# Expert tiles spread over the scan units: nine per chunk of eight, in a loop written out

## What is computed

```python
# branch 1: tokens sorted by nearest of 8 means, then a selective scan (d = 256 channels, 16 states)
dA = exp(d_t[..., None] * A)
h  = dA * h + (d_t * u_t)[..., None] * b_t[:, None, :]     # one step per token, state (256, 16)
y  = einsum('bdn,bn->bd', h, c_t)                          # then + D * u, and tokens put back in place
# branch 2: 8 experts, each token goes to 2 of them
logits = xt @ w_gate; top_logits, sel = top_k(logits, 2); probs = softmax(top_logits)
h = silu(xt @ w1[e]) * (xt @ w3[e]);  y = h @ w2[e];  out += probs * y
```

## Time and profile before

| | |
|---|---|
| median of 3 runs | 818.53 us (818.16 to 818.74) |
| profiled execution | 817.38 us |
| its span, first to last instruction | 815.3 us |
| busy over the span | PE 663.9 us (81%), DVE 682.9 (84%), POOL 597.3 (73%), ACT 431.0 (53%) |
| mean granted clock of TensorE | 0.913 of full speed |
| DMA | 118.63 MB, mean 146 GB/s |

### The profile page before, as it was taken

One profiled execution on the slowest core, in us unless ns is written; L12 is line 12 of the kernel. 1 busy time (PEld: TensorE's weight loads), 2 busy tenths in 40 slices (PEclk: granted clock), 3 DMA queues, 4 the chain that ended last, 5 costly groups with the idle time before them and its releaser, 6 DMA issues. The chain is left out here.

```text
span 815.3 us, 15751 instructions
## 1 busy us (share of the span) xinstructions
PE 663.9 (81%) x4538; PEld 422.7 (52%) x4539; DVE 682.9 (84%) x882; ACT 431.0 (53%) x926; POOL 597.3 (73%) x372
## 2 busy tenths in 40 slices
PE   3734889788998798989998898999889798989870
PEld 2523745245655465556655565565556555655550
DVE  5769777579999999999999999999999999997110
ACT  1324656465655556656655575566557554653320
POOL 3728800038788898988989898888989898889532
PEclk9866955599999989999999998999999998999995
DMA  7972659979944754674575466547645654662322
GB/s 228 371 259 91 180 206 297 321 221 241 210 102 103 144 118 87 146 150 94 115 163 111 89 149 138 105 90 164 139 90 125 134 127 90 142 142 35 49 27 26
DMA packets 76845, 118.63 MB, mean 146 GB/s; under 512 B 22456, under 2 KB 56848, under 8 KB 74512
## 3 DMA queue, kind: packets, MB, share of 16 engines
q1 hardware_dynamic: 54656, 90.95, 41.2%
q0 software_dynamic: 19824, 27.16, 19.4%
q10 hardware_dynamic: 2336, 0.15, 0.2%
HBM read 82.87 MB, written 35.27 MB: 145 GB/s over the span
## 5 line engine op out<-in xcount | busy, mean ns | idle before, releaser
L534 POOL TENSOR_TENSOR ring<-ring,bc 128x1024 f32<-128x1024 f32 (+2 forms) x128 | 308.0, 2424 | 38.9 <-DVE state L1047 38.0
L1044 DVE TENSOR_TENSOR_SCAN ring<-ring,state,pb 128x512 f32<-128x512 f32 x256 | 313.8, 1267 | 4.6
L654 ACT ACTIVATE ring<-late,aneg 128x512 f32<-128x512 f32 x256 | 164.2, 721 | 12.0 <-DMA late<-dd_d 9.1
L1035 DVE TENSOR_TENSOR pb<-fb,bc 128x1024 f32<-128x1024 f32 x128 | 157.3, 1229 | 3.0
L1284 PE MATMUL py<-w2x,pool 128*128 x568 | 141.6, 395 | 0.5 <-ACT pool L726 0.3
L1267 PE MATMUL fa<-w,pool 128*128 x284 | 137.7, 608 | 3.9 <-issue 2.8
L506 POOL DMA_INDIRECT out_dram<-pool,meta x71 | 112.9, 1590 | 29.8 <-issue 15.7
L1267 PE MATMUL fb<-w,pool 128*128 x284 | 134.3, 596 | 0.0
L486 POOL DMA_INDIRECT pool<-xn_d,meta x71 | 71.3, 1004 | 81.3 <-DVE ids L1001 33.5
L1284 PEld LDWEIGHTS py<-w2x,pool 128*128 128x128 f32 x568 | 107.7, 200 | 13.6 <-issue 1.0
L1267 PEld LDWEIGHTS fb<-w,pool 128*128 128x128 f32 x284 | 54.5, 192 | 68.9 <-issue 68.9
(11 more groups left out here) (213 smaller groups left out, 752.8 us busy)
## 6 DMA issues: line engine op xcount, KB each, us to landing
late<-dd_d SPq DMA_DIRECT2D x256, 128.0 KB
bc<-bc_d SPq DMA_DIRECT2D x72, 256.0 KB
w<-in_L_ffn_w_dram SPq DMA_DIRECT2D x16, 512.0 KB, 8.6
ring<-in_L_attn_x_dram SPq DMA_DIRECT2D x8, 512.0 KB, 4.3
out_dram<-ring SPq DMA_DIRECT2D x8, 512.0 KB, 7.7
xn_d<-w2x SPq DMA_DIRECT2D x8, 512.0 KB, 8.6
dd_d<-pool SPq DMA_DIRECT2D x8, 512.0 KB
dd_d<-ring SPq DMA_DIRECT2D x8, 512.0 KB, 5.1
```

What stands on the lines that cost most here:

```text
L534: ins = po.tensor_tensor(r, r, c_rows, ALU.mult)
L654: ins = ac.activation(ring[:, g % RING, n, :], dd[:, g % 2, 0, :], ACT.Exp, scale=aneg[:, NH * g + n:NH * g + n + 1])
L1035: ve.tensor_tensor(pb[:, :].rearrange("p (n c) -> p n c", n=2), pd[:, :].rearrange("p (o c) -> p o c", o=1).to_broadcast([P, 2, CH]), b_ro ...
L1044: ve.tensor_tensor_scan(r, r, pb[:, CH * m:CH * m + CH], state[:, NH * g + n:NH * g + n + 1], ALU.mult, ALU.add).then_inc(S["scan_done"], 1)
```

## The change

It takes the tiles into the units. Chunk 0 has tiles 0 to 7: unit 0 goes first and alone, units 1 to 7 have one tile each and unit 7 a second one in its middle, between its two halves on DVE. Each later chunk has nine tiles: one per unit and a second one in unit 3. So tile 70 belongs to unit 63 and none is left behind. Gathers run six tiles ahead instead of four (`XR`), `ye` has three buffers instead of two (`YE`), `ya` has two and replaces the copy into `yb`. The table's entries are loaded nine at a time. POOL adds two tiles in unit 5 of a chunk (`DOUBLE`), with the second gather and add between the halves of its multiplication. Half of the last unit's multiplication goes to DVE. Chunk 7's scan adds are issued together behind the last tile's. All loops of the stage are written out, with constants as semaphore targets. The first unit's exponentials wait for DVE's preparation to end and for their own load only; those of units 1 and 2 wait for the stores of the last factors, whose buffers they overwrite.

```diff
-SCAN_STEPS = (3, 3, 7, 7)
-REST_SCAN_STEPS = (1, 2, 3, 4)
-REST = range(SPI * NCH + 1, FT)
+UNITS = NCH * G
+SCAN_UNITS = {3: (0, 1), 7: (2, 3)}
+DOUBLE = 5
+XR, XT, YE = 6, 4, 3
+BLOCK = G + 1
...
+        def first_tile(u):
+            c, g = u // G, u % G
+            return u - 1 if c == 0 else BLOCK * c - 1 + g + (g >= G // 2)
+        def middle_tile(u):
+            c, g = u // G, u % G
+            if c == 0:
+                return u if g == G - 1 else None
+            return BLOCK * c + G // 2 - 1 if g == G // 2 - 1 else None
+        def experts_by(u):
+            c, g = u // G, u % G
+            return max(0, u - 1) if c == 0 else BLOCK * c - 1 + g + (g >= DOUBLE)
...
 POOL
+            for u in range(UNITS):
+                c, g = u // G, u % G
+                here = range(experts_by(u - 1) if u else 0, experts_by(u))
+                if len(here) and here[0] + XR < FT:
+                    gather(here[0] + XR)
+                scans = SCAN_UNITS.get(g, ()) if c else ()
+                split = 1 if scans else NH // 2
+                po.wait_ge(S["h_ready"], u + 1)
+                done = multiply(u, slice(0, split))
+                for n in scans:
+                    add_scan(c - 1, n, landed_scan(c - 1, scans[0]) - 16)
+                if len(here) == 2:
+                    add_expert(here[0])
+                    if here[1] + XR < FT:
+                        gather(here[1] + XR)
+                if u < UNITS - 1:
+                    done = multiply(u, slice(split, NH))
+                elif split < NH // 2:
+                    done = multiply(u, slice(split, NH // 2))
+                done.then_inc(S["hc_done"], 1)
+                if len(here):
+                    add_expert(here[-1])
+            add_expert(FT - 1)
+            for n in range(TPC):
+                add_scan(NCH - 1, n, landed_expert(FT - 1))
...
 ACT
+                if u == 0:
+                    ac.wait_ge(S["pr_du"], KC * NCH)
+                elif u == 1:
+                    ac.wait_ge(S["bc_put1"], 32 * NCH // 2)
+                    ac.wait_ge(S["dd_put10"], 16 * NCH // 2)
...
-            evac_xt(0, 0)
-            tanh(0, 0)
-            evac_xt(1, 1)
+            exps(0)
+            put_du(0)
+            evac_xt(0)
+            exps(1)
+            for u in range(1, UNITS):
+                j = first_tile(u)
+                tanh(j)
+                put_du(u)
+                if j:
                     evac_ht(j - 1)
...
+                if j + 1 < FT:
+                    evac_xt(j + 1)
+                if u + 1 < UNITS:
+                    exps(u + 1)
+                if j:
+                    evac_y(j - 1)
+                j = middle_tile(u)
+                if j is not None:
+                    tanh(j)
+                    evac_ht(j - 1)
+                    evac_xt(j + 1)
+                    evac_y(j - 1)
...
 DVE
-            silu(0, 0)
+            for u in range(UNITS):
+                if u:
+                    silu(first_tile(u))
+                half_unit(u, 0)
+                if middle_tile(u) is not None:
+                    silu(middle_tile(u))
+                half_unit(u, 1)
+                keep_states(u)
...
+            ve.wait_ge(S["h_ready"], UNITS)
+            r = ring[:, last_u % RING, NH // 2:NH, :].rearrange("p n c -> p (n c)")
+            ve.tensor_tensor(r, r, bc[:, last_u // G % 2, 1, NH // 2:NH, :].rearrange("p n c -> p (n c)"),
+                             ALU.mult).then_inc(S["hc_last"], 1)
...
 PE
-            pe.wait_ge(S["pr_de"], KC * NCH)
+            pe.wait_ge(S["pr_ab"], KC * NCH)
+            pe.wait_ge(S["pr_re"], KC * NCH)
...
+            for u in range(2, UNITS):
+                j = first_tile(u)
+                up(j, e_up)
+                turn_h(j - 1)
+                pe.wait_ge(S["ye_done"], j)
+                if u >= 3:
+                    turn_y(u - 3)
+                fold_states(u - 2)
+                pe.wait_ge(S["ht_done"], j)
+                if j + 1 < FT:
+                    turn_x(j + 1)
...
+                down(j - 1, e_down)
+                j = middle_tile(u)
+                if j is not None:
+                    up(j, e_up)
+                    turn_h(j - 1)
+                    pe.wait_ge(S["ht_done"], j)
+                    turn_x(j + 1)
+                    pe.wait_ge(S["ye_done"], j)
+                    down(j - 1, e_down)
...
```

More of the change, by code:

```diff
@@ L243, in apart, with scans_by, unit_of_expert, landed_expert @@
             eng.sem_inc(S["passed"], 1)
[L245 to L265, removed]
+        def first_tile(u):
[9 more added lines that the diff above has]
+            return max(0, u - 1) if c == 0 else BLOCK * c - 1 + g + (g >= DOUBLE)
+        def scans_by(u):
+            c, g = u // G, u % G
+            return 0 if c == 0 else (c - 1) * TPC + sum(len(SCAN_UNITS[k]) for k in SCAN_UNITS if k <= g)
+        def unit_of_expert(j):
+            return next((u for u in range(UNITS) if experts_by(u) > j), UNITS - 1)
+        def landed_expert(j):
+            return 16 * (1 + j + 1 + scans_by(unit_of_expert(j)))
+        def landed_scan(c, n):
+            u = (c + 1) * G + next(k for k in SCAN_UNITS if n in SCAN_UNITS[k])
+            return 16 * (1 + experts_by(u - 1) + c * TPC + n + 1)
+        assert first_tile(UNITS - 1) == FT - 1 and experts_by(UNITS - 1) == FT - 1
         @block.sync
@@ L491, in _ @@
             po.wait_ge(S["pr_ids"], NCH - 1)
[L492 to L493 removed]
+            gather(0)
+            gather(1)
             for h in range(KC):
                 po.wait_ge(S[f"dd_put0{h}"], 16 * NCH // 2)
[L496 to L507 removed]
@@ L509, in add_scan @@
-            def add_scan(turn, c, n, beside=0):
-                po.wait_ge(S["yb_done"], c + 1)
-                if not isinstance(c, int):
-                    apart(po)
-                po.wait_ge(S["added"], landed(turn - 1 - beside))
-                apart(po)
-                po.indirect_dma_start(out[:, :], bass.IndirectOffsetOnAxis(ap=idb[:, n:n + 1], axis=0), yb[:, n, :], None,
-                                      compute_op=ALU.add).then_inc(S["added"], 16)
-            po.wait_ge(S["acc_put"], 16 * NCH)
@@ L541, in _ @@
-            turn(0)
-            with po.Fori(1, NCH) as c:
-                turn(c)
-            for i, (kind, n) in enumerate(REST_ADDS):
-                if kind == "expert":
-                    if n + 4 < FT:
-                        gather(n + 4, (n + 4) % SPI)
-                    add_expert(REST_TURN + i, n, n % SPI, n % 2)
-                else:
-                    add_scan(REST_TURN + i, NCH - 1, n)
-            po.wait_ge(S["added"], landed(REST_TURN + len(REST_ADDS) - 1))
+            for j in range(2, XR):
+                gather(j)
@@ L674, in hand_over @@
[L674 to L685 removed]
+                if g == 0 and c >= 2:
+                    ac.wait_ge(S["added"], landed_scan(c - 2, TPC - 1))
@@ L724, in evac_ht, with evac_y @@
             def evac_ht(j):
                 ac.wait_ge(S["htr_done"], j + 1)
+                if j == 0:
+                    ac.wait_ge(S["bc_put0"], 32 * NCH // 2)
                 ac.copy(ht, pt[:, :]).then_inc(S["ht_done"], 1)
-            def evac_y(j, parity, slot, turn):
+            def evac_y(j):
                 ac.wait_ge(S["w2_done"], j + 1)
-                if turn is not None:
-                    ac.wait_ge(S["added"], landed(turn))
-                ac.activation(ye[:, parity, :], py[:, 0:D], ACT.Copy, scale=meta[:, slot, 1:2]).then_inc(S["ye_done"], 1)
```

484 lines of the change are left out of this document (179 added, 305 removed).

## The result

| | before | after |
|---|---|---|
| median | 818.63 us (818.16 to 823.47, 4 runs) | 844.18 us (838.40 to 845.78, 4 runs) |
| profiled execution, its span | 817.38, 815.3 us | 838.40, 836.5 us |
| busy: PE, DVE, POOL, ACT | 663.9, 682.9, 597.3, 431.0 us | 667.7, 682.7, 596.3, 420.0 us |
| mean granted clock | 0.913 | 0.897 |

The changed kernel is slower: the ratio is 1.0286, with a 95% interval of 1.0221 to 1.035. 813 us were predicted, in a range of 799 to 823. The busy time of PE, DVE and POOL is the same to within 1% (ACT has 11 us less), so the time went into waiting.

The account below looks back on a forecast made before the run. DVE was taken to set the pace until 747.1 us, then POOL's chain of adds. Start at 170.0, six periods of 77.2, scans' end 773.1 and tail 33.2 gave span 806.3; clock falls 810, step to median 3.2: 813 us, range 799 to 823.

Parts of the forecast that it names:

- Start: First units on DVE: exponentials no longer wait for all factor stores, unit 1 begins at 170.0, 8.4 us gained.
- SP: SP's queue in the chunks: the removed waits per tile lay beside other work, so nothing was taken for them.
- The cycle of a chunk: Chunks with nine tiles: 77.2 us each, with 4.3 us of DVE stall and PE waiting for POOL after units 5 and 7.
- the offsets: Time from DVE's start of a unit to PE's start of the next unit's `up`; up to 5.9 us DVE waits for nothing.
- The clock: Granted clock falling after PE's waits for POOL: two falls of about 2 us taken, span 806.3 to 810.
- Rival B: Slower: PE's cycle grows further behind units 5 and 7 by clock falls or a second wait; 827 us, chance 0.25.
- the two readings of the clock: PE's clock: first, busier PE leaves no fall, sum 809.5; second, idle gaps throttle again, each chunk's wait may bring a fall.
- Unit 2's factors: Load sharing DMA time with two experts' weights: hidden if landed by 178, some us lost if not.
- The tail: From the scans' end to the kernel's end: 33.2 us instead of 68.2, chunk 7's four scan adds going together.
- the prediction's shared port: Last unit: two-input SBUF DVE operation and POOL exclude each other; POOL's last multiplication could start 1.2 us later, sum 814.

Follow-up runs that it names:

- the later load: Changed kernel with SP's load of the next nine table entries behind unit 4's factor loads instead of unit 3's: 816.48 us, ratio 1.007; again 817.08 us, 1.0107.
- the second profile of the changed kernel: The changed kernel run again with no edit, on another chip: 848.87 us, ratio 1.0397 to the kernel before.
- the filler: Against the later load, PE does four more products that nobody reads, ahead of the sums of units 5 and 7: 810.32 us, ratio 1.0029.
- the written-out loop: The kernel before with only its loops over chunks 1 to 7 written out, constants in place of registers: 815.56 us, ratio 0.9949.
- the best kernel: Against the split in the middle, POOL's double tile in unit 3 instead of 4, single scan adds in units 5 and 7: 802.13 us, ratio 0.982.
- the kernel with no tile moved: The kernel before with loops written out and the last chunk's four scan adds issued together: 800.14 us, ratio 0.9888.
- the split in the middle: Later load, POOL's adds moved, unit 2's factors ahead of weights; now POOL multiplies two states, not one, before scan adds (last unit excepted): 799.05 us, ratio 0.9875.

## Why the prediction was wrong

Point by point, against the changed kernel's profiled execution:

- **Start: right.** Unit 1 begins at 169.0, not 170.0 (164.0 to 169.0 in the other profiles of the same code).
- **SP: the step that failed.** "SP's waits per tile ... lay beside other work on engines with room; I take nothing for it." The text looked at the waits that the change removes. It did not follow the one that it adds: the kernel before loads the table's entries tile by tile and waits for no add there, the new one waits for the landing of the ninth tile's, with unit 4's factors queued behind it. Units 3 and 4 took 177.6 us in the seven chunks where 162.1 were forecast, and 162.0 with the later load. So the later load took 15.5 us off chunks 1 to 7 by profile (566.9 to 551.4), and 2.2 to 2.9% off the ratios. Of ACT's 27.2 us of waiting that is the part that reaches DVE. In the second profile of the changed kernel (575.0 us for chunks 1 to 7) it is more: 23.7 us over the later load's 551.3, 18.2 of them in units 3 and 4.
- **The cycle of a chunk: right, in mechanism and size.** 77.2 was reckoned from the offsets; with the later load and the clock kept up it is 76.9 to 77.7 in five of chunks 2 to 7. Chunk 1, for which the sum has 75.1, took 76.8. The waits stood where they were put: DVE in units 3 and 4 (23.3 us where 23.4 were reckoned), PE for POOL behind units 5 and 7. So the waits of PE for POOL were no surprise, and what they do to the clock is the next point.
- **The clock: undersized, the second step that failed.** Two falls of 2 us were taken, with "PE has fewer other gaps". There were eight, and about 1.3 us each with the later load (with the filler seven of its eight were gone, and 8.8 us with them). The price of one was overrated, the number underrated by four times. The reading that it rests on, that the five falls before sit behind waits of PE for POOL, holds for four (waits of 2.04 to 3.27 us); the fifth, at 684 us, has only gaps of 1.27, 0.44 and 0.68 us ahead of it. Rival B was right in its mechanism: with the later load chunks 2 to 7 take 1.9 us each over the forecast, above the 1.5 from which it decides, and the filler takes 1.5 of these away. (Its 2.8 us per chunk are 17 us in six chunks, which on 813 would be 830, not 827.) Of the two readings of the clock that the prediction weighed, the second holds: idle gaps bring the clock down. With the later load PE is busy for 90% of chunks 1 to 7, against 89% before, and the clock falls eight times instead of five.
- **Unit 2's factors: the condition was put wrongly.** The load was called hidden if it landed by 178. It landed at 177.3 and cost 2.44 us. Behind it ACT still has 2.5 us of exponentials and 0.6 of tanh before DVE, which was ready at 178.0; it had to land by 174.9.
- **The tail: right.** 33.1 for 33.2. The last add was issued 23.8 us behind the scans' end (24.5 reckoned). Two errors cancel in it: POOL begins the last unit 0.2 us behind DVE's last instruction instead of 2.3, and its product ahead of the first two adds takes 1.0 us longer than reckoned, a delay that the prediction put at 1.2 us, outside of its sum (last section).

The sum: 1.8 in chunk 0 (unit 2's stall, less the earlier start), 15.5 for SP's wait, 8.8 for the clock, 4.2 of other excess in the chunks (538.4 against 542.6 with the filler, half of it its one fall) make the 30.3 us by which the scans end late. The attributions to single edits come from different chips and carry a few us of scatter; chunk 0, which the later load doesn't touch, ends at 236.7 us in the changed kernel's profile and at 230.3 in the later load's. The median's excess over 813 is 31.2 us: 4.5 more come from the step from the profile's span to the median, 7.7 us where 3.2 were taken, and the 4 us that the forecast had taken for the clock go off.

Why did the large rearrangement move so little even without its fault? A ninth tile costs a chunk 77.5 - 71.8 = 5.7 us (the filler's kernel against the written-out loop, mean of seven chunks), 40 us for seven. A tile in the tail cost (68.2 - 33.1)/6 = 5.9 us, 35 us for six, with some 5 us in it that belong to the adds let go together. Three engines were near full already, so there was no room in the units for the tile to go to; it only changed places. What the change brings in earnest are its small parts: the start, the loop, the adds let go together. The last two alone, with no tile moved, reach 0.9888. That the tiles in the units add anything is not shown, even for the best kernel (0.982), since it has the new start as well, and no run has the new start with the tiles left behind. On chip 7 the kernel with no tile moved took 800.14 us and the one with the split in the middle 799.05, though unit 1 begins 7.5 us earlier in the latter (166.33 against 173.84): the rest of the change, the moved tiles among it, gave all but 1.1 us of that back.

## What to carry to other kernels

An engine that issues loads in order is a queue like any other: when a wait moves or its target comes later, list what is queued behind it and who needs that, even if what it waits for is needed by nobody. Before work is moved from a tail into a full stage, add up each engine there: with three near 90% or above, a tile costs in the stage what it cost behind it. Where an engine has to be late once per turn, place it where the one who waits is late as well, and look at what clock the wait leaves behind.

## What the hardware showed that was not expected

DVE takes half of the last unit's multiplication, two inputs in SBUF (1.23 us at 803.59, the same length as its product from PSUM). POOL's product over 128x512 went beside it; the same form four units earlier stands above it:

```profile
766.05 1.26 POOL L489 TENSOR_TENSOR ring<-ring,bc 128x512 f32<-128x512 f32 x1 [4.08 <-DVE state L997]
...
803.64 2.29 POOL L489 TENSOR_TENSOR ring<-ring,bc 128x512 f32<-128x512 f32 x1 [2.50 <-DVE state L997]
806.10 1.58 POOL L483 DMA_INDIRECT out_dram<-late,ids  x1 [0.16 <-issue]
807.98 1.56 POOL L483 DMA_INDIRECT out_dram<-late,ids  x1 [0.30 <-issue]
...
812.60 1.58 POOL L476 DMA_INDIRECT out_dram<-pool,meta  x1 [1.76 <-DMA out_dram<-late,ids]
```

It took 2.29 us, against 1.26 and 1.28: 1.0 us more, close to the length of DVE's instruction. It is what the prediction's shared port would do, and the best kernel shows it again (2.30 us at 766.90). By these rows its 1.0 us lies on the chain that sets the end: the first add follows the product at once, and the next tile's add waits for the landing of these two. No run here took DVE's half away, so what it costs in all is not shown.

The clock's falls needed no long idleness. With the later load all eight stand behind single waits of PE for POOL of 2.0 to 3.3 us, while four waits of 1.7 to 2.2 us had none behind them. Length alone doesn't decide it: with the split in the middle a wait of 2.87 us, in chunk 2, brought no fall. Four products of no use ahead of such waits kept all but one away. The 6.2 us that they gave stand on one comparison; but from chunk 2 on the lengths of the chunks, 76.9 to 77.7 with the filler, and 78.4 to 80.5 and 78.1 to 79.6 in the two profiles without it, do not overlap, except for the one with the fall (79.5).
